# Inverse's landing on a semaphore of its own, and floor's loads moved ahead in SyncE's list

## What is computed

```python
q = (query @ Wq + bq);  k = (key_value @ Wk + bk);  v = (key_value @ Wv + bv)   # split in 16 heads of 16
attn = jnp.einsum('bhqd,bhkd->bhqk', q, k) * scale
attn = jnp.clip(attn, -CLAMP, CLAMP)
attn = jax.nn.softmax(attn, axis=-1)
x = jnp.einsum('bhqk,bhkd->bqhd', attn, v).reshape(B, Nq, Cq)
return x @ Wo + bo
...
x = x + _L0_xattn_ref(_layernorm(x, axis=-1), ctx_768, ...)
x = x + _L0_ffn_ref(...)      # experts, top 2 of 8, and a shared one
x = x + _L1_xattn_ref(...)    # ternary weights, int8 activations
x = x + _L1_ffn_ref(...)      # a cell scanned over 16 steps, then tanh
```

## Time and profile before

| | |
|---|---|
| median of 3 runs | 1038.03 us |
| the profiled execution | 1038.37 us |
| its span in the profile | 1036.3 us |
| TensorE matmul, busy | 840.0 us, 81% |
| VectorE, busy | 716.6 us, 69% |
| ScalarE, busy | 540.5 us, 52% |
| GpSimd, busy | 272.4 us, 26% |
| mean granted clock of TensorE | 0.883 |
| first and last clip of the attention | 61.2 and 394.2 us |

### The profile page before, as it was taken

The page is one execution under the profiler, slowest core; times in us unless marked ns, Lnnn a source line. Parts: engine busy times, 40 slices in busy tenths (PEclk is TensorE's granted clock), DMA queues, the critical chain, the costliest instruction groups (busy, mean ns, idle before and its releaser), DMA issues.

```text
span 1036.3 us, 22061 instructions
## 1 busy us (share of the span) xinstructions
PE 840.0 (81%) x7942; PEld 617.7 (60%) x7942; DVE 716.6 (69%) x1496; ACT 540.5 (52%) x1179; POOL 272.4 (26%) x236
## 2 busy tenths in 40 slices
PE   3778787887778677779989999997655989778995
PEld 2355555655555455557747777774222767548995
DVE  7678676766556479876666676654798575776866
ACT  3345455554445233643356556536987464574542
POOL 2256342342222040504041111003723000063300
PEclk9979999999889777799999999997558797898998
DMA  6444455555655344732345566344210000200001
GB/s 172 110 106 106 116 138 123 119 129 114 123 129 122 87 119 144 235 108 77 87 117 163 159 201 194 110 124 138 74 37 1 1 1 0 81 2 1 3 1 65
DMA packets 81630, 102.02 MB, mean 98 GB/s; under 512 B 22934, under 2 KB 65713, under 8 KB 81482
## 3 DMA queue, kind: packets, MB, share of 16 engines
q1 hardware_dynamic: 73162, 92.41, 33.7%
q0 software_dynamic: 6144, 7.42, 2.7%
q10 hardware_dynamic: 2256, 1.29, 0.5%
HBM read 85.66 MB, written 15.19 MB: 97 GB/s over the span
## 4 chain that ended last, share of the span: by engine, by line
PE 38%; DMA 25%; DVE 19%; issue 7%; ACT 5%; POOL 3%; SPq 2%; ACTq 0%; DVEq 0%; POOLq 0%
PE ps L1176 10%; DMA rden<-inverse 9%; PE ps L1163 7%; DMA xe<-floor 6%; DMA floor<-floor_q 5%; PE ps L1680 3%; DMA q_parts<-qp 3%; PE ps L2124 2%; PE ps L1674 2%; PE ps L2135 1%; DVE pmax L1641 1%; PE ps L1669 1%; ACT area L1930 1%; DMA stage<-in_L_xattn_W_f_dram 1%; DVE m L499 1%
## 5 line engine op out<-in xcount | busy, mean ns | idle before, releaser
L499 DVE TENSOR_REDUCE m<-ps 100x2 f32<-100x722 f32 x128 | 114.9, 901 | 61.0 <-PE ps L494 60.7
L534 DVE SCALAR_TENSOR_TENSOR p<-p,xe 121x600 f32<-121x600 f32 x128 | 104.5, 817 | 53.4 <-DMA xe<-floor 48.5
L1225 ACT ACTIVATE hT<-ps,cols 128x500 f32<-128x500 f32 (+1 forms) x96 | 62.5, 651 | 106.7 <-PE ps L1163 98.6
L519 ACT ACTIVATE p<-ps 121x600 f32<-121x600 f32 x128 | 85.0, 664 | 58.5 <-PE ps L512 56.2
L1176 PE MATMUL ps<-w_h,hT_h 128*125 128x256 f16 (+1 forms) x384 | 105.9, 276 | 7.4 <-DVE x L1272 6.8
L1176 PE MATMUL ps<-w_l,hT_h 128*125 128x256 f16 (+1 forms) x384 | 105.8, 276 | 0.0
L1176 PE MATMUL ps<-w_h,hT_l 128*125 128x256 f16 (+1 forms) x384 | 105.8, 276 | 0.0
L1232 DVE TENSOR_TENSOR hT_l<-hT,hT_h 128x500 f16<-128x500 f32 (+1 forms) x96 | 62.3, 651 | 61.7 <-ACT hT_h L1226 61.7
L512 PE MATMUL ps<-qs,ks 128*121 128x100 f16 x768 | 73.2, 238 | 14.7 <-ACT p L519 8.4
L512 PEld LDWEIGHTS ps<-qs,ks 128*121 128x121 f16 x768 | 65.8, 153 | 31.8 <-ACT p L519 17.4
L1068 POOL DMA_INDIRECT xe<-tokens,slot_of x32 | 43.1, 1347 | 155.3 <-PE ps L1186 102.1
(11 more groups left out here) (340 smaller groups left out, 2181.8 us busy)
## 6 DMA issues: line engine op xcount, KB each, us to landing
xe<-floor SPq DMA_DIRECT2D x32, 378.1 KB
sw<-in_L_ffn_w_dram SPq DMA_DIRECT2D x16, 512.0 KB, 6.3
sw<-in_L_ffn_w_dram SPq DMA_DIRECT2D x8, 1024.0 KB, 5.8
stage<-in_L_xattn_W_f_dram SPq DMA_DIRECT2D x6, 1024.0 KB, 7.4
k_parts<-kp SPq DMA_DIRECT2D x32, 181.5 KB, 5.0
ks<-k_parts SPq DMA_DIRECT2D x32, 181.5 KB
ctx_f<-in_ctxT_dram SPq DMA_DIRECT2D x16, 270.8 KB, 6.0
stage<-in_ctxT_dram SPq DMA_DIRECT2D x8, 541.5 KB, 8.4
```

The lines of the kernel that those rows point to most:

```text
L499: v.tensor_reduce(m32[p][:, 2 * i:2 * i + 2], ps[0:T, at:at + 2, 0:KV], AX.X, ALU.max).then_inc(m_max, 1)
L519: s.activation(p32[:, i % HALF, :, :, :].rearrange("p j n t -> p n j t"), ps[0:KT, t_bank(i):t_bank(i) + 2, 0:KJ * T].rearrange("p n (j t) ...
L534: v.scalar_tensor_tensor(probs, probs, 1.0, low, ALU.min, ALU.max).then_inc(a_cv, 1)
L1225: s.activation(hT[:, f % 3, 0:m], bank[2 + f % 2][:, 0:m], ACT.Silu, bias=bias, scale=1.0 / WS)
```

## The change

The broadcast of the inverse gets a semaphore of its own, rden_in, which GpSimd waits for; den_dma counts 32 for a batch, the den load and the inverse's store. The den load of a batch thereby waits for the landing of the inverse's store of the batch before, and no more for that of the broadcast. In SyncE's list, floor load half 1 stands ahead of the den load, and floor load half 0 of the next batch ahead of the inverse's store.

```diff
-        den_dma = sem("den_dma")
+        den_dma, rden_in = sem("den_dma"), sem("rden_in")
@@ den_load
             sp.wait_ge(o_32, b + 1)
             wait(sp, o_r, b)
-            wait(sp, den_dma, 48 * b)
+            wait(sp, den_dma, 32 * b)
             sp.dma_start(den[:, :], o32[p][D:128:HR, :]
                          ).then_inc(den_dma, 16)
 
         def inv_vector(v, b):
-            v.wait_ge(den_dma, 48 * b + 16)
+            v.wait_ge(den_dma, 32 * b + 16)
@@ inv_load
-            sp.wait_ge(den_dma, 48 * b + 32)
+            sp.wait_ge(den_dma, 32 * b + 32)
             wait(sp, o_n, b)
             sp.dma_start(rden[:, :],
-                         inv_d[:, None, :].broadcast_to((QUAD, HR, HG * T))).then_inc(den_dma, 16)
+                         inv_d[:, None, :].broadcast_to((QUAD, HR, HG * T))).then_inc(rden_in, 16)
 
         def on_gpsimd(g, b, p):
-            g.wait_ge(den_dma, 48 * (b + 1))
+            g.wait_ge(rden_in, 16 * (b + 1))
@@ a_sync
                 k_store(sp, b + 2, t + 1, p, 0)
+            floor_load(sp, b, 1)
             if b >= 1:
                 den_load(sp, b - 1, q)
-            floor_load(sp, b, 1)
@@
                 floor_store(sp, b + 1, 0)
+            if has(b, 1):
+                floor_load(sp, b + 1, 0)
             if b >= 1:
                 inv_store(sp, b - 1)
-            if has(b, 1):
-                floor_load(sp, b + 1, 0)
             if not has(b, 2):
                 inv_load(sp, b - 1)
```

## The result

The changed kernel takes 1028.3 us (median of 7 runs, 1023.0 to 1030.3), the kernel before 1038.0 us (7 runs on the same chip, 1032.4 to 1042.4): a ratio of 0.990, 95% interval [0.987, 0.993]. It is 1.0% faster, and the forecast of no change (1038.0 us, range 1031.5 to 1043.5) was wrong. The profiled execution took 1029.8 us (span 1027.7).

The account below looks back on a forecast made before the run. The attention loop was taken as paced by SyncE's list and transfers. Terms -5.8 - 0.4 + 4.2 + 2.1 = +0.1 us on the profiled 1038.37 us gave, on the median, 1038.0 us, range 1031.5 to 1043.5.

Parts of the forecast that it names:

- what L1 waits for next: Attention loop: floor load half 1 next waits for its own store, landing at 188.0, and goes 0.55 us earlier.
- rival D: Attention loop: floor store half 1 lands long before the broadcast, its load goes 4.8 us earlier; 998 us, chance 0.04.
- Part 1: Attention loop, 12 rounds: floor load half 1 ahead of the denominators, without the wait on the broadcast, gains 5.8 us.
- Part 2: Attention loop: floor load half 0 ahead of the inverse's store shifts later issues 0.38 us in 11 rounds, costing 4.2 us.
- rival B: Attention loop: the inverse store's shift is absorbed by the backlog and Part 1's gain passes whole; 1032 us, chance 0.17.
- rival C: Attention loop: the inverse's store, behind floor load half 0, gates the broadcast, costing 6.3 us; 1044 us, chance 0.25.
- the pass-on of 87%: Steady rounds: some 87% of floor load half 1's gain reaches the next floor load half 0, 0.48 us a round.
- Part 3: End of the loop: the broadcast waits for the inverse store's landing, so batch 15's floor load half 1 costs 2.1 us.
- Part 2's 0.4 us in batch 3: Batch 3: floor load half 0 had waited for the reciprocal; going ahead of the inverse's store gains about 0.4 us.

Follow-up runs that it names:

- s1_ahead: sem_only with floor store half 1 issued ahead of the broadcast instead of behind it: ratio 0.974, 1003.9 us.
- s1_ahead_before: The kernel before with only floor store half 1 and the broadcast exchanged, one semaphore kept: ratio 0.999.
- den_late: sem_only, but the den load waits for floor store half 1's landing and so stands directly ahead of floor load half 1: ratio 1.003.
- one_piece: sem_only plus one 64-byte transfer directly ahead of floor load half 1, once floor store half 1 has landed: ratio 0.994.
- den_twice: den_late with the den load issued a second time, into a tile that nothing reads: ratio 1.014.
- l0_first: The kernel before with the next batch's floor load half 0 ahead of the inverse's store, nothing else: ratio 1.000.
- s1_l1_first: s1_ahead with floor load half 1 also put directly ahead of the den load: ratio 0.978.
- tail_old: The changed kernel with the old order of floor load half 0 and the inverse's store in batch 14's round alone: ratio 0.9885.
- sem_only: The kernel before with the broadcast's own semaphore alone, SyncE's list as before: ratio 0.988.
- after_again: The changed kernel run again unchanged, against the kernel before: ratio 0.992.
- order_only: The kernel before with both moves in SyncE's list but still one shared semaphore: ratio 0.9925.
- before_again: The kernel before run again unchanged: ratio 0.9998.
- sem_again: The same kernel as sem_only, run on another chip: ratio 0.988.
- s1_ahead_den_late: s1_ahead with the den load moved behind the first halves of k and q: ratio 0.978.

## Why the prediction was wrong

**Right: what L1 waits for next.** The prediction put its own store in the broadcast's place, landed at 188.0, and L1 0.55 us earlier. By its last increment S1 landed at 188.03. Measured: 144.0 us of waits of L486 on the floor's stores, L1 0.02 us behind S1, 0.53 us gained, and not the 4.8 us of rival D. s1_ahead and s1_ahead_before and the increments show the mechanism, four of S1's pieces held up behind the broadcast's. That the semaphore by itself is idle once L1 stands ahead of the den load was not said.

**Failed: Part 1's L1 of unchanged duration.** The sum moved L1 and the denominators landed "at 192.5 (188.03 + 4.45)": L1 kept its 4.45 us. It takes 3.83 us when nothing is issued directly ahead of it. This is 0.76 us a round, more than the 0.55 us that was counted. The L1 of batch 2 is shorter by 2.8 us even; that is not the den load's doing, since den_late has 4.56 us there, and its cause was not looked for. den_late separates the steady rounds' lengthening from the wait for the broadcast, which it doesn't have; one_piece and den_twice show that it needs more than one piece ahead (0.2 us for that) and does not grow from 100 rows to 200. The rows to see it were at hand: L0, the same load of 378 KB with the den load long gone, took 3.70 us, and the only row of an L1 directly behind a den load 4.45 us. The prediction used both and never asked why they differ.

**Failed: Part 2's shift of 0.38 us in 11 rounds (4.2 us).** It rested on the broadcast's constant 6.5 to 6.7 us from its issue, read as a landing that follows the issue. Two rows were too few. With L0 first, the broadcast goes 4.07 to 4.10 us behind L0 (before 3.39 to 3.44): a shift of 0.65 us, more than the 0.38 that was charged. But from there to S1's landing it is 5.92 us in l0_first and 6.31 and 5.89 in the kernel after, 6.81 to 6.83 before. So the landing of S1 follows what was queued from L0 on and not the broadcast's issue; rival B's first half. l0_first at 1.000 bounds what is left of the charge: at most 0.3%, 3 us, and by its mean nothing; and this holds the cost at the end of the loop too. In the kernel after the sum L0 to S1 landed was 10.39 in one profile and 9.98 in the other (before 10.27, 10.20), which doesn't tell a few tenths from zero.

**Right: rival C's price, not its place.** The wait of the broadcast for the inverse's store came. Of its 12.8 us some 7 lie in the rounds of batches 3 to 13, for which C put the price at 6.3 us; the rest is at the end of the loop. It is part of the 0.65 us of later issue, and it was absorbed like the rest. C failed because S1's landing does not follow the broadcast's issue.

**Mis-sized: the pass-on of 87%.** The time from L1's landing to the next L0 grew from 4.44 to 5.04 us, so of the 0.53 + 0.76 = 1.29 us by which L1 lands earlier after S1, 0.60 is given back: 53% passes on, and with the 0.05 us between L0 and S1 a round is 0.75 us shorter (19.83 to 19.08, means of two). The 87% was taken from where the issue of other transfers moves and L1 does not. Most of the 0.60 us is S0's own time, from 4.50 and 4.23 us to 5.00 and 4.68; the reading, not tested by a run of its own, is that what was issued behind L1 (den load, k, q, context) is not done earlier by as much, and S0 waits behind it. The 5.65 us of s1_l1_first in that place are of another kind: S0 takes 4.17 us there, and is issued 1.47 us late.

**Right: Part 3.** 2.1 us forecast; 2.3 us by SyncE's rows of after against tail_old, some 2.6 us by the means of the landings (37.2 against 34.6, kernels with the wait for the broadcast gone). From the last L0 to the last L1 it is 13.25 us, just over the forecast 11.5 to 13. Its worth in time was not separable from scatter.

**Right too: Part 2's 0.4 us in batch 3.** There L0 went 0.74 and 0.67 us behind S0's landing before and 0.02 us after.

**The sum redone** with the measured terms: 11 rounds of 0.75 us are 8.3; the L1 of batch 2 gives 2.8 - 0.76 = 2.0 more; the last L1, of batch 13, 1.29 whole: 11.6 us, against 12.2 by the landings (249.6 to 237.4, means of two). The end costs 2.3 us, of which the shorter rounds of batches 14 and 15 bring back about half, so that 1.1 us remain (39.6 to 40.7): 10.5 us by the sum, 11.0 by the landings, 9.7 measured in time. The three rounds from L0 of batch 10 to that of batch 13 gained a little more (23.18 and 22.95 us each before, 22.33 and 22.00 after). The first profile of after, by contrast, lost 7 us in a stretch (690 to 780 us) that the change doesn't touch and that no other profile repeats.

**Open:** why a load of 100 rows directly ahead makes all pieces of the next load later, 0.5 to 0.8 us in all; and whether sem_only, at 0.988 twice against 0.990 to 0.9925 for after, after_again and order_only, is truly the better kernel; the intervals overlap, and the end's 2.3 us alone is as large as the difference.

## What to carry to other kernels

Before a small transfer is moved to another place in a queue, count what it does to the transfer behind it and not only its own issue: the same load at two places of a round with two durations (3.7 and 4.45 us here) is a row to explain, not a constant. When a wait of a transfer falls, ask which large transfer was queued ahead of it: exchanging two lines, so that the store of 8 rows of 100 values went ahead of the 200 KB broadcast, was worth 1.4% on top of the semaphore, and nothing without it. An issue that moves later is only charged if the landings behind it are shown to follow issues, in more than two rows.

## What the runs showed of the hardware

- A 378 KB load (121 partitions of 3200 bytes) takes 3.8 us from issue to landing with nothing issued close ahead on its queue (after, after_again, order_only), 4.4 to 4.8 us right behind a load of 100 rows (before, before_again, den_late, den_twice; batches 4 to 8), and 4.30 us right behind a single piece of 64 bytes against 4.06 without it (one_piece, sem_only and sem_again; medians of batches 3 to 13). With the 200 KB broadcast still under way seven of its eleven pieces are on time and four late, 4.3 to 4.5 us in all (s1_ahead_den_late, s1_l1_first). By the Trainium skill ("DMA: Bandwidth & Descriptors", "Anatomy of one DMA", a fit for transfers that GpSimd issues) it would be about 2.0 us plus 378 KB over 436 GB/s = 2.9 us, an estimate that lies below all of these.
- A store of the floor took 2.05 us with little ahead of it, and 5.2 to 6.2 us (means of batches 4 to 8) issued 0.65 us behind a 200 KB broadcast, four of its eight pieces landing just behind the broadcast's four. Issued ahead of the broadcast it takes 3.6 to 3.8 us, and its landing comes 2.4 us earlier in the round.
